# Attention stacks read from DRAM with a repeated source, and another order of work where projections end

## The reference

```python
def _L0_attn_ref(x, ocr_context, Wq, bq, Wk, bk, Wv, bv, Wo, bo, ocr_bias):
    q = x @ Wq.T + bq + ocr_bias
    k = x @ Wk.T + bk
    v = x @ Wv.T + bv
    ...
    scores = jnp.einsum('bhsd,bhtd->bhst', q, k) / math.sqrt(HEAD_DIM)
    scores = scores + _band_mask(S, scores.dtype)
    attn = jax.nn.softmax(scores, axis=-1)
    out = jnp.einsum('bhst,bhtd->bhsd', attn, v)
    ...

def _reference_tuple_inner(x, W_dq, W_uq, W_dkv, W_uk, W_uv, W_o):
    ...
    attn = jnp.einsum('bhql,bkl->bhqk', q_lat, c_kv) / sqrt(hs)
    attn = jnp.where(causal[None, None], attn, -jnp.inf)
    attn = jax.nn.softmax(attn, axis=-1)
    ...

x = x + 0.5 * _L0_ffn_ref(_layernorm(x, axis=-1), ...)
x = x + _L0_attn_ref(_layernorm(x, axis=-1), ...)
x = x + 0.5 * _L0_ffn_ref(_layernorm(x, axis=-1), ...)
x = x + 0.5 * _L1_ffn_ref(_layernorm(x, axis=-1), ...)
x = x + _L1_attn_ref(_layernorm(x, axis=-1), ...)
x = x + 0.5 * _L1_ffn_ref(_layernorm(x, axis=-1), ...)
```

## Time and profile before

| | us |
|---|---|
| median of 3 runs | 599.3 |
| lowest and highest | 596.71, 599.79 |
| the profiled execution | 597.05 |
| its span | 595.5 |
| mean granted TensorE clock | 0.884 |

### The profile page before, as it was taken

The page is one execution under the profiler, slowest core; times in us unless marked ns, Lnnn a source line. Parts: engine busy times, 40 slices in busy tenths (PEclk is TensorE's granted clock), DMA queues, the critical chain, the costliest instruction groups (busy, mean ns, idle before and its releaser), DMA issues. The chain is left out here.

```text
span 595.5 us, 12830 instructions
## 1 busy us (share of the span) xinstructions
PE 465.0 (78%) x4453; PEld 341.7 (57%) x4453; DVE 390.8 (66%) x1003; ACT 307.5 (52%) x559; POOL 221.3 (37%) x396
## 2 busy tenths in 40 slices
PE   1766576799999999688467757579999998766775
PEld 0545342467777776466235544358878787534554
DVE  6889667467777773687477756665766676246872
ACT  4543363256566667574666415414555555766631
POOL 6355463111111112130788534410222222269851
PEclk9979776589999999699779968857999999968995
DMA  5000078533332210000000003792333331000001
GB/s 161 1 1 0 1 209 214 163 82 82 70 65 78 76 42 4 0 2 1 0 1 1 1 0 106 202 263 60 84 83 81 84 92 29 3 0 0 19 20 35
DMA packets 40228, 35.98 MB, mean 60 GB/s; under 512 B 5872, under 2 KB 35440, under 8 KB 40176
## 3 DMA queue, kind: packets, MB, share of 16 engines
q1 hardware_dynamic: 40176, 35.32, 22.7%
HBM read 21.28 MB, written 13.63 MB: 59 GB/s over the span
## 5 line engine op out<-in xcount | busy, mean ns | idle before, releaser
L626 ACT ACTIVATE h_sb<-psum 128x1024 f32<-128x1024 f32 (+1 forms) x128 | 114.9, 916 | 91.3 <-PE psum L565 48.4
L651 DVE TENSOR_REDUCE nm<-psum 128x2 f32<-128x512 f32 x128 | 82.5, 687 | 32.6 <-PE psum L535 31.3
L654 DVE TENSOR_REDUCE nm<-psum 128x3 f32<-128x384 f32 x128 | 66.3, 554 | 35.8 <-PE psum L541 35.4
L672 POOL TENSOR_TENSOR nmb<-nm,zero 128x16 bf16<-128x16 f32 x32 | 7.0, 220 | 156.5 <-DVE nm L651 90.4
L939 PE MATMUL psum<-wgT,fxT 128*128 128x352 f32 x64 | 27.5, 559 | 27.6 <-ACT fxT L1004 27.6
L227 POOL TENSOR_TENSOR rstd<-veps,mhalf 128x4 f32<-128x4 f32 (+1 forms) x32 | 29.3, 915 | 46.2 <-DVE veps L213 44.8
L270 PE MATMUL psum<-h_sb,dw 128*128 128x256 f32 x176 | 44.7, 408 | 0.0
L234 PE MATMUL psum<-ident,xn 128*128 128x128 f32 x64 | 13.7, 352 | 38.7 <-DVE xn L221 27.4
L578 PE MATMUL psum<-h_sb,v_b 128*32 128x256 f32 x512 | 41.7, 398 | 0.2
L534 PE MATMUL psum<-kst,qst 72*128 72x256 bf16 x128 | 35.5, 299 | 4.9 <-DMA kst<-k_dram 3.0
L270 PEld LDWEIGHTS psum<-h_sb,dw 128*128 128x128 f32 x176 | 34.6, 203 | 8.0 <-issue 2.8
(11 more groups left out here) (227 smaller groups left out, 1478.9 us busy)
## 6 DMA issues: line engine op xcount, KB each, us to landing
q_dram<-q_parts SPq DMA_DIRECT2D x48, 192.0 KB, 3.3
qst<-q_dram SPq DMA_DIRECT2D x32, 288.0 KB
kst<-k_dram SPq DMA_DIRECT2D x96, 96.0 KB
k_dram<-k_parts SPq DMA_DIRECT2D x16, 192.0 KB, 3.5
qst<-nmT SPq DMA_DIRECT2D x96, 4.0 KB, 1.7
x<-in_L_attn_x SPq DMA_DIRECT2D x4, 256.0 KB, 4.5
out_x<-x SPq DMA_DIRECT2D x4, 256.0 KB, 2.3
pk<-in_packed SPq DMA_DIRECT2D x1, 689.5 KB, 6.1
```

The source lines that it names most:

```text
L626: nc.scalar.activation(pexp[p][:, :, 0:w], psum[:, 4 + 2 * (p % 2):6 + 2 * (p % 2), 0:w], ACT.Exp, scale=scale).then_inc(sem("a_exp"), 1)
L651: nc.vector.tensor_reduce(nm[slot % 2][:, h], bank[e].rearrange("p (t k) -> p t k", t=2), AX.X, ALU.max, negate=True).then_inc(sem("a_max" ...
L654: nc.vector.tensor_reduce(nm3[slot % 2][:, h], bank[e][:, 0:3 * P].rearrange("p (t k) -> p t k", t=3), AX.X, ALU.max, negate=True).then_in ...
```

## The change

The query parts are saved once, without the repeated axis. A stack is still four transfers, but now `kst` is one transfer of 72 rows whose source names its 24 rows three times with step 0, and `qst` is three of 24 rows whose source names 8 rows three times. The end of the projections is one routine, `entrance`, for both layers. The line numbers of `sp_save` and `sp_stack` stay nearly the same; L506 is then the load of `kst` and L509 that of `qst`.

```diff
-        q_dram = nc.dram_tensor("q_dram", (2, B, NPART, NPART, HD, H, S), bf16).ap()
+        q_dram = nc.dram_tensor("q_dram", (2, B, NPART, HD, H, S), bf16).ap()
...
-        NSAVE = 16 * 2 * (NPART + 1)
+        NSAVE = 16 * 2 * 2
...
-                    for j in range(NPART):
-                        sp.dma_start(q_dram[inst, el, :, j].rearrange("a i d h t -> (a d h) i t"), parts[0][u % 4][:, e]).then_inc(sem(f"p_dram{u % 4}"), 16)
-                    sp.dma_start(k_dram[inst, el].rearrange("a j d h t -> (a d h) j t"), parts[1][u % 4][:, e]).then_inc(sem(f"p_dram{u % 4}"), 16)
+                    for dram, part in ((q_dram, parts[0]), (k_dram, parts[1])):
+                        sp.dma_start(dram[inst, el].rearrange("a i d h t -> (a d h) i t"), part[u % 4][:, e]).then_inc(sem(f"p_dram{u % 4}"), 16)
...
-                sp.dma_start(qst[slot][0:NQK], q_dram[inst, el, :, :, :, hs].rearrange("a i j d h t -> (a i j d) h t")).then_inc(sem(f"a_stack{slot}"), 16)
+                k = k_dram[inst, el, :, :, hs].rearrange("a j d h t -> a (j d) (h t)").to_broadcast([NPART, NPART * HD, HH * S])
+                sp.dma_start(kst[slot][0:NQK], k).then_inc(sem(f"a_stack{slot}"), 16)
                 for i in range(NPART):
-                    r = slice(i * NPART * HD, (i + 1) * NPART * HD)
-                    sp.dma_start(kst[slot][r], k_dram[inst, el, :, :, hs].rearrange("a j d h t -> (a j d) h t")).then_inc(sem(f"a_stack{slot}"), 16)
+                    q = q_dram[inst, el, i, :, hs].rearrange("a d h t -> a d (h t)").to_broadcast([NPART, HD, HH * S])
+                    sp.dma_start(qst[slot][i * NPART * HD:(i + 1) * NPART * HD], q).then_inc(sem(f"a_stack{slot}"), 16)
...
-            def front(eng, which):
+            def front(eng, which, slot):
...
+            def entrance(ph, at):
+
+                if ph is proj_a:
+                    run(ph, 2, 3)
+                at["prefetch"](eng, which)
+                run(ph, 3, 5)
+                if which in ("pe", "dve"):
+                    at["front"](eng, which, 0)
+                    run(ph, 5, 6)
+                    at["front"](eng, which, 1)
+                elif which == "sp":
+                    at["front"](eng, which, 1)
+                    run(ph, 5, 6)
+                else:
+                    run(ph, 5, 6)
+                    at["front"](eng, which, 0)
+                    at["front"](eng, which, 1)
...
-            run(proj_a, 2, 4)
-            attn_a["prefetch"](eng, which)
-            run(proj_a, 4, 6)
+            entrance(proj_a, attn_a)
...
-            run(proj_b, 3, 4)
-            attn_b["prefetch"](eng, which)
-            run(proj_b, 4, 6)
+            entrance(proj_b, attn_b)
```

More of the change, by code:

```diff
@@ L795, in prefetch @@
                         sp_stack(eng, q0, slot)
-            def front(eng, which):
[L799 to L813, removed]
+            def front(eng, which, slot):
+                if slot == 0:
+                    for name, v in {"pe": [("p_v", 4 * inst + 4), ("p_qf", 4 * inst + 4), ("p_kf", 4 * inst + 4)],
+                                    "pool": [("p_v", 4 * inst + 4)]}.get(which, []):
+                        eng.wait_ge(sem(name), v)
+                if which == "pe":
+                    for p in range(PR):
+                        pe_scores(eng, q0, slot, p)
+                        if slot == 1 and p == 1:
+                            pe_maxT(eng, q0, 0)
+                if which == "dve":
+                    for p in range(PR):
+                        dve_max(eng, q0, slot, p)
+                    if not l0:
+                        dve_causal(eng, q0, slot)
+                if which == "sp" and slot == 1:
                     sp_rows(eng, q0, 0)
-                if which == "act":
+                if which == "act" and slot == 1:
                     act_maxT(eng, q0, 0)
                 if which == "pool":
-                    pool_vb(eng, q0, 0)
-                    for slot in range(2):
-                        pool_split(eng, q0, slot)
+                    if slot == 0:
+                        pool_vb(eng, q0, 0)
+                    pool_split(eng, q0, slot)
             def quad(eng, which, n, beside):
@@ L1329, in attention @@
             def attention(at, beside):
-                at["front"](eng, which)
                 for n in (0, 1, 3):
```

## The result

| | before | changed |
|---|---|---|
| median of the runs, us | 599.5 (4 runs) | 654.0 (4 runs) |
| lowest and highest | 596.71, 602.94 | 646.98, 659.59 |
| the profiled execution, its span | 597.05, 595.5 | 646.98, 645.2 |
| mean granted TensorE clock | 0.884 | 0.858 |

The changed kernel is slower: its time is 1.0873 times the time before, with a 95% interval of 1.0791 to 1.0956; its slowest run, 659.59 us, counts as a slow one and is left out of this ratio. The forecast was 630 us, with a range of 600 to 700. The sum was made for the span: 32.5 us forecast, 645.2 - 595.5 = 49.7 measured.

A forecast was written before the change was run, and what follows sets the result against it. TensorE bounded steady attention and a chain the entrances. Slower stacks then add 11.3 + 18.4 us in steady units and 0.4 + 2.4 at entrances: 32.5 on 597.05 gives 629.6, say 630 us, range 600 to 700.

The forecast's parts named there:

- Three engines: Stack transfers, with 3 copies outermost in the source, use 3 of 16 DMA engines: share near 0.19.
- T: Time of one stack on three engines, taken as 8.5 us, with 12.2 us kept for the range.
- The rival that stacks keep their speed: Rival, chance 0.17: stacks move as fast as before, the new order gains 8.6 us, total 588.5 us.
- The entrances: Where projections give way to attention: the new order's gain is eaten by slow stacks, +0.4 and +2.4 us.
- The 11.0 us between the first two in the sum: First entrance: the last save and stack 3 add 11.0 us after L554, so the second unit starts at 123.0.
- The order part: Earlier stacks, maxima and rows at both entrances: with stacks as fast as before, gains 5.3 and 3.3 us.
- the first L534 would start near 93.4: Sign at the first entrance that the order part is right: scores start when DVE has finished v.
- the rows of slot 0 would leave within 0.1 us of nmT: Sign that the order part is right: at the entrances these rows leave before the last save.
- The unit of 8.8: Steady attention: a unit lasts 8.8 us, against 7.9 and 7.3 before in the two phases.
- 7.45 + 1.7 + T: Two steady units: unit start to stack issue, fixed part of a small transfer, then T; 17.65 us.
- the +11.3 and +18.4: Loss over twelve steady units in the first and second phase: 105.9 us against 94.6 and 87.5.
- the clock in a rival: Rival, chance 0.20 shared with crowded engines: holes in each unit keep TensorE at clock 0.50, total 665 us.

The follow-up runs named there:

- experiment 1: Changed kernel with stack rows reordered so the q source's repeat stands inside (outermost 24 for q, 8 for k): 589.5 us, ratio 0.9832 to the kernel before.
- experiment 9: Changed kernel with 16 overwritten matmuls before every stack wait but the first two of each phase: 634.3 us, ratio 1.0543 to the kernel before.
- experiment 10: Changed kernel with 24 overwritten matmuls before every stack wait but the first two of each phase: 632.6 us, ratio 1.0548 to the kernel before.
- experiment 2: Changed kernel with k loaded as before (24 plain rows three times), q still with the repeat outermost: 596.5 us, ratio 0.9889 to the kernel before.
- experiment 5: Changed kernel, its transfers and saves kept, with the program order of the kernel before: 657.4 us, ratio 1.0956 to the kernel before.
- experiment 7: Changed kernel with stacks 4 to 15 of each phase loading only six of eight heads: 616.5 us, ratio 1.0187 to the kernel before.
- experiment 8: Changed kernel with 60 overwritten matmuls before the stack wait of odd slots, first phase only: 653.5 us, ratio 1.0817 to the kernel before.
- experiment 3: Changed kernel with experiment 1's transfers, query parts saved once, and the order of the kernel before: 593.5 us, ratio 0.9860 to the kernel before.
- experiment 4: Changed kernel's new order with all transfers and saves of the kernel before: 593.7 us, ratio 0.9869 to the kernel before.
- experiment 6: Changed kernel with stacks 4 to 15 of each phase loading only four of eight heads: 605.3 us, ratio 1.0056 to the kernel before.

## Why the forecast was right in kind and short in size

**Three engines: right.** 0.19 of 16 engines, as forecast, and 72 to 81 GB/s where 65 to 75 was written. T is 7.3 to 8.2 us instead of 8.5. That the order of the sizes sets it, and not the repeat as such, is shown for q by experiment 1. The rival that stacks keep their speed falls; its time, 588.5, is what experiment 1 gives with another order of rows (589.5).

**The entrances: right.** Rows against forecast: L554 at 111.75 for 112.0, second unit at 123.60 for 123.0, no change instead of +2.4 in the second phase. The 11.0 us between the first two in the sum, a save and a stack, agree with the measured 11.8 by luck: TensorE waited only 0.5 us for a stack there and otherwise worked at a clock of 0.50, as in the 10.96 us before. The order part was taken at 106.4 with stacks there in time, and experiment 1 has 105.85; its gain in the second phase, from the last unit of the first to L561, is 4.5 (164.5 for 169.0) where 3.3 was written. Two of the things I said would show it were off: I wrote that the first L534 would start near 93.4 and it started at 94.48, and that the rows of slot 0 would leave within 0.1 us of nmT. They left at 107.73, though ACT had nmT at 103.2, since the saves of the second and third step stood in SP's way, single issues of which took up to 3.6 us (97.30) where they take 0.5 otherwise, behind three stacks on the way.

**The unit of 8.8: the step that failed.** I wrote "So two units last 7.45 + 1.7 + T = 17.65", at both phases, with waits of "1 to 1.5 us each" in nearly every unit, and the +11.3 and +18.4 hang on it: 29.7 us, where 49.8 were measured. Measured: 20.0 and 18.6 for two units. Its parts in the pair at 185.99: 9.34 instead of 7.45 from the start of the unit to the issue, 10.05 instead of 10.2 from the issue to the first scores, and 0.56 from there to the next start, which I had left out. In the clean pair at 492.50 they are 6.18, 10.87 and 0.59, so my 7.45, read in one unit, was long there by as much as the other two were short. That such pairs came out near 17.65 is luck for a second reason. From 492 to 519 the share is 0.20, no less than in stretches in which only a stack moves, at 70 GB/s: the three engines hardly pause, and at that rate the two stacks and two sets of rows of a pair, 1204 KB, need 17.2 us by themselves. There the engines' rate is the bound, beside the chain of a single stack that I added up; in the pair at 185.99 they stood at a share of 0.06 from 192.5 to 197 instead, waiting for the late issue.

What was wrong is the assumption behind the sum, that the waits are short and the clock stays up. The slack of a pair is one or two waits; where it is one of 3.5 us, TensorE's clock falls to 0.50, the unit behind it is late with nmT by some 1.6 us, its stack goes out late, and the next wait is as long again. Experiments 9 and 10 bear this out: with shorter waits two units last 17.5 us on average in the second phase of experiment 10 and 18.2 in its first, where TensorE's own work with the filler is the bound, and the total is 632.6, near the 629.6 of the sum. I had weighed the clock in a rival, with "the holes, about a microsecond of nine, are shorter than the idle before 95.85" against it. The mean hole was right (12.5 + 18.1 us over 24 units are 1.3 each); that the holes gather in every second unit was not seen. The rival's own picture, a clock at 0.50 throughout and 665 us, was too dark: the means are 0.88 and 0.92.

The Trainium skill (TensorE: Matmul & The Clock Gate, Part 1: The HAM clock gate (the "warmup" mystery)) says that the gate goes by how busy the engine has been of late. By that rule the trace agrees: 1.00 in the steady units of experiment 10, with no wait for a stack over 0.8 us, and 0.50 behind the 3.52 us.

**What stays open.** Which pattern an execution falls into, and why the first phase of the changed kernel stays in the uneven one for all twelve units while the second changes between both, no run settles; the spread of its total, 647 to 660, may be that. How the missing 1.2 and 0.5 us of a unit divide between the late rows, SP's longer issue of them (2.71 us at 192.02, 1.84 at 200.08) and transfers that queue behind each other was not measured apart either, and no run kept the clock up with the long waits left in.

## What to carry to other kernels

Before a load is rewritten with a repeated source, look at which size of the access pattern stands outermost: the same bytes moved at 139 to 156 GB/s or at 78 by the order of the sizes, and the repeat can stand inside. And where a producer is slower than the engine it feeds by less than a unit's work, don't only compare means: ask where the wait collects, since an engine may run slower after one long wait, as TensorE did here, and so delay the next request.

## What the runs showed of the hardware that I had not expected

A few hundred useless matmuls made a kernel faster: 24 of them, 1.51 us, before each stack wait brought 654.0 to 632.6 us, with the clock at 1.00 in both phases. The wait's length alone does not tell whether the clock falls: behind 2.17 and 1.34 us in the rows above it stayed at 1.00 from 501 to 510, and behind the 1.97 us before 518.54 it was 0.66 from 519 to 524.

A small transfer beside slow ones on a few engines takes longer: by the profiles' medians the rows of nmT land after 2.2 or 2.3 us in the changed kernel and in experiments 2, 5 and 7 to 10, against 1.7 or 1.8 in the kernel before, in experiments 1, 3 and 4, and with half of the bytes (experiment 6). A stack waits behind the one before it too: from its first issue to its use it takes 10.05 us where the engines had been at a share of 0.06, and 10.87 in the pair at 492.50, where they hardly pause.
